# Four masks braided into one: the side on which ScalarE's copy jumps, in the inverse of a row sort

## The reference

```
x = x + dct(gn(x))            # masked 2-D DCT, two channels only
x = x + patches(gn(x))        # 5x5 neighbourhood weighted by cosine similarity
x = x + gate(gn(x))           # channel gate from the mean of a phase-only image
x = x + sorted_attention(gn(x))
```

```
xh   = first 16 channels, sorted along h, then along w (idx_h, idx_w kept)
qkv  = conv1x1(depthwise 3x3, 5x5, 7x7 of conv1x1(x))   -> q1, k1, q2, k2, v
idx  = argsort(v) over all 3136 pixels of a channel
q1, k1, q2, k2, v gathered by idx -> two attentions over the sorted pixels
out1, out2 put back in place (inverse of idx); out = conv1x1(out1 * out2)
first 16 channels: inverse of idx_w, then inverse of idx_h
```

## Time and profile before

| | |
|---|---|
| time, median of 3 runs | 17144.38 us (17140.89 to 17151.51) |
| the profiled execution's own time | 17148.49 us |
| its span in the trace | 17146.6 us |
| VectorE busy | 16016.6 us, 93% of the span |
| ScalarE busy | 7247.1 us, 42% |
| TensorE matmuls busy | 6760.6 us, 39% |
| the inverse of the row sort: first to last braid | 14219.98 to 16441.86 us |
| braids (line 1497) | 156 instructions, 966.6 us |

### The profile page before, as it was taken

The page is one execution under the profiler, slowest core; times in us unless marked ns, Lnnn a source line. Parts: engine busy times, 40 slices in busy tenths (PEclk is TensorE's granted clock), DMA queues, the critical chain, the costliest instruction groups (busy, mean ns, idle before and its releaser), DMA issues.

```text
span 17146.6 us, 106420 instructions
## 1 busy us (share of the span) xinstructions
PE 6760.6 (39%) x40644; PEld 2812.9 (16%) x40644; DVE 16016.6 (93%) x10433; ACT 7247.1 (42%) x5055; POOL 0.2 (0%) x4
## 2 busy tenths in 40 slices
PE   6888855570025614613722632642561101210010
PEld 4444431120011111201211211211111000000000
DVE  6999988899999999999999999999999998879978
ACT  0000003343453453444444444345345337868854
POOL 0000000000000000000000000000000000000000
PEclk9999987785567757856866866875775555555555
DMA  0000012110001000000100100100100001131232
GB/s 18 13 25 17 21 37 71 54 31 11 10 10 31 23 10 26 27 10 22 31 10 10 40 15 10 35 19 10 31 23 10 25 14 41 52 86 51 71 73 65
DMA packets 297993, 509.96 MB, mean 30 GB/s; under 512 B 54685, under 2 KB 258685, under 8 KB 287413
## 3 DMA queue, kind: packets, MB, share of 16 engines
q1 hardware_dynamic: 297460, 502.90, 10.3%
HBM read 298.39 MB, written 204.33 MB: 29 GB/s over the span
## 4 chain that ended last, share of the span: by engine, by line
DVE 60%; issue 10%; ACT 6%; PE 3%; DMA 1%; SPq 1%; DVEq 0%; ACTq 0%
DVE arena L1070 21%; DVE arena L1077 15%; DVE arena L1054 5%; DVE masks L1046 5%; DVE arena L1061 5%; DVE arena L1550 3%; PE psum L1332 2%; ACT arena L1497 2%; DVE arena L1548 2%; ACT arena L1020 2%; DVE arena L1401 1%; ACT arena L1507 1%; DMA masks<-row_masks 1%; ACT arena L1010 1%; DVE arena L1407 1%
## 5 line engine op out<-in xcount | busy, mean ns | idle before, releaser
L1020 ACT ACTIVATE arena<-arena 128x4096 f32<-128x4096 f32 (+26 forms) x1456 | 3072.3, 2127 | 5883.2 <-DVE arena L1077 5883.0
L951 PE MATMUL psum<-arena,wt 128*32 128x448 f32 x31360 | 3379.9, 594 | 1873.0 <-ACT arena L967 1126.7
L1070 DVE COPY_PREDICATED arena<-masks,arena 128x4096 f32<-128x4096 uint8 (+26 forms) x1456 | 4017.3, 2787 | 9.3 <-ACT arena L1020 9.3
L1077 DVE COPY_PREDICATED arena<-masks,arena 128x4096 f32<-128x4096 uint8 (+26 forms) x1456 | 4001.3, 2775 | 0.6
L951 PEld LDWEIGHTS psum<-arena,wt 128*32 128x32 f32 x31360 | 1047.2, 119 | 4208.2 <-issue 2660.3
L1287 PE MATMUL psum<-ident,arena 128*112 128x128 f32 x896 | 194.4, 386 | 3557.8 <-ACT arena L1208 2826.6
L1550 DVE COPY_PREDICATED arena<-arena 128x2048 f32<-128x2048 uint8 (+28 forms) x364 | 972.2, 2687 | 241.8 <-ACT arena L1507 241.6
L1046 DVE TENSOR_TENSOR masks<-arena 128x1568 uint8<-128x1568 f32 (+21 forms) x912 | 1033.9, 1192 | 128.9 <-ACT arena L1010 128.9
L731 PE MATMUL psum<-arena 128*128 128x392 f32 x3072 | 1053.8, 496 | 31.9 <-DVE arena L633 31.8
L1054 DVE TENSOR_TENSOR arena<-arena 128x1568 f32<-128x1568 f32 (+21 forms) x912 | 1056.3, 1220 | 0.0
L1061 DVE TENSOR_TENSOR arena<-arena 128x1568 f32<-128x1568 f32 (+21 forms) x912 | 1037.6, 1197 | 0.3
(11 more groups left out here) (126 smaller groups left out, 6794.2 us busy)
## 6 DMA issues: line engine op xcount, KB each, us to landing
arena<-xpad SPq DMA_DIRECT2D x896, 108.5 KB, 2.4
xpad<-arena SPq DMA_DIRECT2D x8, 1924.0 KB, 7.0
arena<-in_x SPq DMA_DIRECT2D x8, 1568.0 KB, 10.4
x3d<-arena SPq DMA_DIRECT2D x8, 1568.0 KB, 5.2
prodd<-arena SPq DMA_DIRECT2D x8, 1568.0 KB, 5.2
arena<-prodd SPq DMA_DIRECT2D x8, 1568.0 KB, 13.8
arena<-x3d SPq DMA_DIRECT2D x8, 1568.0 KB, 10.1
out<-arena SPq DMA_DIRECT2D x64, 196.0 KB, 4.5
```

The costliest lines, as they stand in the source:

```text
L951: last = nc.tensor.matmul(psum[C * b:C * b + C, n % C_BANKS, 0:CROWS * W], wt[:, g, C * w:C * w + C], cx[i % 2][b][:, y0:y0 + CROWS, x0:x0 ...
L1020: last = nc.scalar.activation(packed_view(ptmp, here, piece, NP), pair_views(pay[b], piece, NP)[0], ACT.Copy)
L1070: last = nc.vector.copy_predicated(lo, wide_mask(q, piece, at), hi)
L1077: last = nc.vector.copy_predicated(hi, wide_mask(q, piece, at), packed_view(ptmp, here, piece, NP))
```

## The change

One access pattern pair of one instruction is rewritten. Each braid moves the same 4n bytes from the same places to the same places. Before, ScalarE walks tile by tile: it reads n bytes of a tile in one run and writes them at every fourth byte. After, it walks pair by pair: it writes the 4n bytes in one run, and each four of them are read from four regions, 1568 bytes apart, then from the next byte of the first.

```
                 n = ROW_NET[SR - 1 - i][2]
-                nc.scalar.activation(um[i % 3][:, 0:NP * n].rearrange("p (n w) -> p w n", w=NP), masks[:, :, 0:n],
+                nc.scalar.activation(um[i % 3][:, 0:NP * n].rearrange("p (n w) -> p n w", w=NP), masks[:, :, 0:n].rearrange("p w n -> p n w"),
                                      ACT.Copy).then_inc(u_mk, 1)
```

## The result

The changed kernel takes 17468.53 us (median of 4 runs, 17465.8 to 17470.5) against 17144.25 us of the kernel before on the same chip. The ratio is 1.0188, with a 95% interval of 1.0171 to 1.0206: slower by 324 us. The forecast was 17494 us, slower.

What follows compares the result with a forecast made beforehand. VectorE leads the chain (60%), but the braid's stage is near balance with ScalarE. ScalarE's 567.8 us of extra work, less waits step by step, leaves 202.4 + 147.5 + 0 = 349.9 us: 17494 us, range 17180 to 17720.

Steps and rivals of the forecast that it cites:

- The balance of the stage: Braid's stage: VectorE and ScalarE close to balance in locked steps; ScalarE waits 276.0 us for VectorE, VectorE 241.6 us for ScalarE.
- The price of the jumping read: New braid on ScalarE: 1.80 ns an element, 11.43 us for 6272 elements, 567.8 us more work over 156 braids.
- The fixed part: Cost of each ScalarE braid apart from its elements: left at 144 ns, as before the change.
- The step-by-step sum: Each of 156 braids' extra time less ScalarE's waits for VectorE until the next braid, not below zero: 349.9 us.
- cover: ScalarE's waits for VectorE between braids, taken to absorb a longer braid; 26 steps with long enough waits leave nothing.
- Waits for masks: Mask transfers between braids: no cover for a longer braid; new waits under 1 us possible, put at zero.
- Free reads: ScalarE's read port: jumping reads cost nothing, one-run write cures the braid, 0.832 ns an element, 72 us faster, 17072 us; chance 0.14.
- Partly hidden jumps: Braid's read: jumps partly hidden, 1.24 to 1.6 ns an element, 17181 to 17356 us; chance 0.14.
- no difference: Braid: both patterns cost the same within 0.1 ns (1.02 to 1.24), 17144 us; chance 0.06.
- Clashes with VectorE: Braid dearer than any row, over 2.05 ns, by byte reads or VectorE memory clashes; 2.1 ns gives 17720 us; chance 0.05.

Runs made afterwards that it cites:

- run 2: Kernel before, with the braid's read jumping 4 bytes at every element within 16 bytes, write in one run, wrong mask bytes: 17055.5 us, ratio 0.9948.
- run 3: Kernel before, with the braid's read jumping 16 bytes at every element, write in one run, wrong mask bytes: 17474.4 us, ratio 1.0195.
- run 4: Kernel before, with the braid reading two adjacent bytes, then jumping 1568, write in one run, wrong mask bytes: 17063.3 us, ratio 0.9955.
- run 12: Kernel before, with the braid reading in runs and its write jumping 8 bytes at every element, wrong mask bytes: 17892.3 us, ratio 1.0435.
- run 1: Kernel before, with the braid copying in runs on both sides, not interleaving, wrong mask bytes: 17052.0 us, ratio 0.9949.
- run 5: Kernel before, with the braid reading in runs and writing at every second byte, wrong mask bytes: 17069.3 us, ratio 0.9951.
- run 6: Kernel before, with the braid reading in runs and its write jumping 4 bytes at every element within 16, wrong mask bytes: 17064.7 us, ratio 0.9949.
- run 9: Whole kernel: kernel before with the braid moving the same bytes to the same places in blocks of four pairs: 17064.2 us, ratio 0.9952.
- run 7: Kernel before, with the braid reading in runs and its write jumping 16 bytes at every element, wrong mask bytes: 19526.6 us, ratio 1.1383.

## Why the prediction was right, step by step

**The balance of the stage.** Right. 276.0 us of spare time and a step that is locked were the two things that made 510 us of extra work cost 324. The other direction fits too: 237 us less bring 82, since VectorE had only 241.6 us of waits to give back, 103 of them in the four waits of the earlier trace rows.

**The price of the jumping read.** Right in its cause, and 6% too high: 1.80 ns taken, 1.694 measured. The fixed part was too low: 144 ns taken, 204 to 304 measured. Together 567.8 us of extra work were forecast, and 510.0 came. The cause, another place for every element, was only argued from the earlier trace rows; runs 2, 3 and 4 show it. The rule of the Trainium skill, page "SBUF — State Buffer", section "Specifications (TRN2)", (16-byte lines, two accesses in each) held for reads in runs 2, 3 and 4 (0.834, 1.717 and 0.860 ns). For byte writes it doesn't hold: two writes in each line still cost 2.25 ns (run 12). The rule of the Trainium skill, page "ScalarE: Activation LUTs", section "What ACT_TABLE_LOAD costs" (0.833 ns an element, no word on the pattern) agrees with the runs whose changes of 16 bytes are hidden (1, 2, 5, 6 and 9) and not with the changed kernel or runs 3, 7 and 12.

**The step-by-step sum.** With the measured durations in place of 1.80 ns it gives 298.5 us; with the price alone wrong the forecast of 349.9 falls by 51. The 156 steps of the two traces, from one braid to the next, grew by 317.6 us:

| steps | sum says | measured |
|---|---|---|
| no wait for VectorE before (52) | 178.5 us | 181.0 us |
| a wait too short (74) | 120.0 us | 117.7 us |
| a wait long enough (30) | 0 | 18.9 us |

The last line is the one step of the argument that failed: a wait isn't always cover. Here is such a step of the changed kernel, the one where the merge level changes and both lots have to be done:

```profile
14436.33 10.94 ACT L1497 ACTIVATE arena<-masks 128x6264 uint8<-128x6264 uint8 x1 [1.16 <-DMA masks<-row_masks]
...
14447.14 2.23 ACT L1507 ACTIVATE arena<-arena 128x2048 f32<-128x2048 f32 x2
14449.40 2.75 DVE L1550 COPY_PREDICATED arena<-arena 128x2048 f32<-128x2048 uint8 x2 [6.26 <-ACT arena L1507]
...
14457.15 2.01 ACT L1507 ACTIVATE arena<-arena 128x2172 f32<-128x2172 f32 x1 [4.88 <-DVE arena L1548]
```

ScalarE waits 4.88 us for VectorE, as it did before (4.87), though its braid is 3.76 us longer. VectorE had itself waited for ScalarE, 6.26 us, and the wait came after it. The step grew by 3.82 us where my sum has zero. Five such steps (two changes of level, the two ends of a round, and one with a long wait of 9.6 us) make 17 us of the 18.9. This is read from the traces; no run was made for it.

**Waits for masks.** Put at zero, measured 112.8 against 102.6 us: 32 waits instead of 24. Right within what the sum can tell.

**The whole.** 298.5 for the steps with the right price, 19.1 for what wasn't cover, is 317.6; the spans differ by 320.8 us and the medians by 324.3. So 51 us too much by the price and 19 us too little by the cover went against each other, and 17494 stood only 25 us too high: that the number came so close is in part luck. One slip in the range had no effect: its lower end is given as "17180 (1.3 ns)", but the prediction's own sum puts 1.3 ns at 57 us, which is 17201; 17180 belongs to 1.24 ns. VectorE's waits were forecast at some 590 us (540.4), ScalarE's at 60 (86.3), and a step of 6144 elements at 16.5 us (16.05).

**The rivals.** *Free reads* is refuted by the changed kernel itself and by run 3, though half of its reasoning is right: the old write was too dear, and curing it brings 81.7 us in run 9 and 89.0 in run 1, where I had put 72. *Partly hidden jumps* and *no difference* are refuted by the price. *Clashes with VectorE* took at most 10 us from VectorE, by which its copies grew, and the braid stayed under the 2.05 ns of that rival.

## What to carry to other kernels

For a copy that reorders small elements, count on each side how many elements in a row fall in the same 16 bytes before choosing the side that jumps, and look for a third order: a small block can keep both sides inside 16 bytes, which neither of two plain loop orders does. Then price the edit step by step by what the other engine waits for, and accept a wait as cover only if the engine waited for wasn't itself held up by yours. A layout that suits the less busy engine is no gain if the busier one must then step through it.

## What was not expected of the hardware

- ScalarE's byte writes cost far more than float writes when each goes to other 16 bytes: 4.17 ns against 1.78 ns, so 26.8 us for 6272 bytes in place of 5.4. Reads of bytes cost 1.69 to 1.72 ns, a little less than those of floats (1.78 to 1.97 ns).
- VectorE's predicated copy takes twice as long (9.6 us against 4.68 for 4220 elements) when its values are reached at a step of two floats, that is with two elements in the same 16 bytes. ScalarE's read of the same values in the same run grows by 8% only (3.99 us against 3.71).
